# Norms of layer 3's expert rows computed beside layer 0's scatters instead of inside layer 3's attention loop

## The reference, cut to what matters

```python
x = x + L0_xattn(layernorm(x), ctx, mask)        # 16 heads of 8
x = x + L0_ffn(layernorm(x))   # self-attention, then 16 experts, top 2, with a capacity of 128 tokens each
x = x + L1_xattn(layernorm(x), ctx)              # 8 heads of 64
x = x + L1_ffn(layernorm(x))                     # two-token attention, 8 experts, top 1
x = x + L2_xattn(layernorm(x), ctx)              # 16 heads of 64, normed queries and keys
x = x + L2_ffn(layernorm(x))                     # self-attention, 8 experts and a shared one
x = x + L3_xattn(layernorm(x), ctx)              # 16 heads of 64
x = x + L3_ffn(layernorm(x))                     # 8 experts with weight norm, top 2
```

```python
def _wn(v, g):
    n = sqrt(sum(v * v, axis=-1)); return v / maximum(n, 1e-12) * g[:, None]
for i in range(8):
    W1, W2 = _wn(w1_v[i], w1_g[i]), _wn(w2_v[i], w2_g[i])   # (512, 128), (128, 512)
    h = (x * mask_i) @ W1.T + b1[i]; h = h * sigmoid(h)
    out += mask_i * (h @ W2.T + b2[i])
```

## Time and profile before

| | us |
|---|---|
| median of 3 runs | 1207.38 (1205.71 to 1211.97) |
| profiled execution | 1199.52 |
| its span | 1197.6 |
| PE busy | 948.9 |
| VectorE (DVE) busy | 559.4 |
| ScalarE (ACT) busy | 440.2 |
| GpSimd (POOL) busy | 241.8 |

### The profile page before, as it was taken

One profiled execution on the slowest core, in us unless ns is written; L12 is line 12 of the kernel. 1 busy time (PEld: TensorE's weight loads), 2 busy tenths in 40 slices (PEclk: granted clock), 3 DMA queues, 4 the chain that ended last, 5 costly groups with the idle time before them and its releaser, 6 DMA issues. The chain is left out here.

```text
span 1197.6 us, 15552 instructions
## 1 busy us (share of the span) xinstructions
PE 948.9 (79%) x5561; PEld 645.1 (54%) x5561; DVE 559.4 (47%) x1292; ACT 440.2 (37%) x769; POOL 241.8 (20%) x283
## 2 busy tenths in 40 slices
PE   6976899525728549999768768998699978869998
PEld 4653445324625336777548733232366677747776
DVE  5865446241236452111766747773354537531111
ACT  2431555302313114343443325766222334323443
POOL 0542301041053000000374334100000013430110
PEclk9986879957968858999998877999899989978999
DMA  8005310104520000110000051300011102100111
GB/s 326 1 14 119 116 46 10 37 26 125 164 70 1 1 0 18 36 35 18 1 1 1 1 132 49 93 21 2 1 40 39 49 18 64 61 1 18 36 35 36
DMA packets 33263, 55.71 MB, mean 47 GB/s; under 512 B 3696, under 2 KB 25397, under 8 KB 32816
## 3 DMA queue, kind: packets, MB, share of 16 engines
q1 hardware_dynamic: 32176, 52.88, 14.5%
q0 software_dynamic: 1024, 1.98, 0.6%
HBM read 44.81 MB, written 9.96 MB: 46 GB/s over the span
## 5 line engine op out<-in xcount | busy, mean ns | idle before, releaser
L2312 PE MATMUL psum<-xT_all,wexp 128*128 128x512 f32 x400 | 184.7, 607 | 1.3 <-issue 0.7
L1511 DVE TENSOR_REDUCE arena<-psum 128x2 f32<-128x1024 f32 (+3 forms) x128 | 127.2, 1021 | 73.5 <-PE psum L2098 46.0
L1058 ACT ACTIVATE arena<-psum 128x512 f32<-128x512 f32 (+3 forms) x256 | 116.1, 516 | 83.8 <-PE psum L2111 45.3
L743 POOL TENSOR_TENSOR rstd<-var,held 128x4 f32<-128x4 f32 (+3 forms) x30 | 54.2, 1820 | 392.7 <-DVE var L1267 372.0
L2312 PEld LDWEIGHTS psum<-xT_all,wexp 128*128 128x128 f32 x400 | 74.6, 196 | 78.8 <-issue 73.8
L2012 PE MATMUL psum<-values_out_all,arena 128*128 128x128 f32 x560 | 80.1, 293 | 36.8 <-ACT arena L1022 27.6
L2327 PEld LDWEIGHTS psum<-wexp,arena 128*128 128x128 f32 x800 | 95.9, 195 | 15.0 <-issue 14.8
L2095 PE MATMUL psum<-arena 72*128 72x512 bf16 (+3 forms) x256 | 83.0, 396 | 24.4 <-DVE arena L1511 11.8
L814 POOL TENSOR_TENSOR arena<-arena,small 128x616 f32<-128x616 f32 x56 | 67.9, 1216 | 147.8 <-DVE small L1451 147.4
L2327 PE MATMUL psum<-wexp,arena 128*128 128x128 f32 x800 | 96.2, 278 | 0.0
L2012 PEld LDWEIGHTS psum<-values_out_all,arena 128*128 128x128 f32 x560 | 70.7, 201 | 45.2 <-ACT arena L1022 35.0
(11 more groups left out here) (288 smaller groups left out, 1426.3 us busy)
## 6 DMA issues: line engine op xcount, KB each, us to landing
wexp<-experts SPq DMA_DIRECT2D x32, 514.0 KB, 3.5
parts_k<-wexp SPq DMA_DIRECT2D x12, 384.0 KB, 2.9
arena<-parts_k SPq DMA_DIRECT2D x48, 96.0 KB
arena<-parts_q SPq DMA_DIRECT2D x48, 96.0 KB
arena<-experts SPq DMA_DIRECT2D x8, 514.0 KB, 3.8
wexp<-experts SPq DMA_DIRECT2D x9, 384.0 KB, 3.1
held<-packed SPq DMA_DIRECT2D x1, 2375.0 KB, 15.4
held<-packed SPq DMA_DIRECT2D x1, 2264.5 KB, 20.3
```

The lines of the kernel that those rows point to most:

```text
L743: pool.tensor_tensor(dst, src, half[0:src.shape[0], 0:n], ALU.pow).then_inc(done, 1)
L1058: act.activation(p_self[:, n % 2, kt % 2, j, lo:S], bank(t_bank("keys", c, k), lo, S), ACT.Exp, scale=DS ** -0.5).then_inc(ut_ok, 1)
L1511: dve.tensor_reduce(top[:, x % 2, qt, j:j + 2], src, AX_X, ALU.max, negate=True).then_inc(us_ok, 1)
L2312: mm(bank(c, 0, BANK), wexp[:, side, c * P:(c + 1) * P], xT_all[:, b * S:(b + 1) * S], start=True, stop=True).then_inc(h_ps, 1)
```

## The change

The eight experts' rows go into layer 0. After the last value matmul of layer 0's self-attention and after the loads of experts 2 and 3, SyncE loads 1024 columns of each of layer 3's eight experts into `rows3`, the first 8192 columns of the arena, by eight DMAs of 512 KB. ScalarE, behind layer 0's gating, waits for all eight (`n_in`), squares them in place and then loads the Gelu table. PE, behind the bias matmuls and the wait for `b2_ok`, sums the squares by the same 64 matmuls, all into bank 7, expert after expert, before it starts on the queues. VectorE takes the two maxima for all experts at once before its first queue; POOL takes three powers behind its 16 scatters. In layer 3's loop squares, sums, maxima and powers are gone, and so are the eight loads before it; experts 0 and 1 are loaded once, at the end of layer 2. The semaphore counts are adapted.

```diff
 # SyncE, layer 0
             for side in range(2, 4):
                 load0(side, side)
+            for e in range(8):
+                sp.dma_start(rows3[:, e, :], experts[3][e][:, 0:1024]).then_inc(n_in, 16)
             sp.wait_ge(scattered, 16 * 16)
...
-                if l == 3:
-
-                    for side in range(2):
-                        sp.wait_ge(ye_ps, 2 + KB[l])
-                        load(l, side, side)
-                    with sp.Fori(0, 3) as i:
-                        for side in range(2):
-                            sp.wait_ge(n_sq, i * 2 + (side + 1))
-                            load(l, i * 2 + (side + 2), side)
-                    sp.wait_ge(n_sq, 8)
-                else:
-                    sp.wait_ge(ye_ps, 2 + KB[l])
+                sp.wait_ge(ye_ps, 2 + KB[l])
...
 # POOL
-            def inverse_norms(n):
-
-                pool.wait_ge(n_max, 2 + 2 * (n + 1))
-                for v in (s1_all[:, 8 * n:8 * n + 8], s2_col[:, 2 * n:2 * n + 2]):
+            def inverse_norms():
+
+                pool.wait_ge(n_max, 1)
+                for v in (s1_all[:, 0:16], s1_all[:, 16:32], s2_col):
                     pool.tensor_tensor(v, v, half[:, 0:v.shape[-1]], ALU.pow).then_inc(n_inv, 1)
...
-                    if l == 3 and n % 4 == 3 and n > 4:
-                        inverse_norms(n // 4 - 1)
-                if l == 3:
-                    inverse_norms(3)
...
                             .then_inc(scattered, 16)
+                inverse_norms()
                 for side in range(4):
...
 # ScalarE
-                def squares(e):
-                    side = e % 2
-                    act.wait_ge(w_in[side], 16 * (e // 2) + 16 * (WB[3][side] + 1))
-                    act.wait_ge(n_ps, e + 1)
-                    act.activation(sq[:, side, :], wexp[:, side, 0:1024], ACT.Square).then_inc(n_sq, 1)
...
-                        if l == 3 and n % 2 == 0:
-                            squares(n // 2)
...
+                for e in range(8):
+                    act.wait_ge(n_in, 16 * 8)
+                    act.activation(rows3[:, e, :], rows3[:, e, :], ACT.Square).then_inc(n_sq, 1)
                 act.preload_act_table(ACT.Gelu)
...
 # VectorE
-                def norms(e):
-                    side = e % 2
-                    dve.wait_ge(n_ps, e + 3)
-                    raw = bank(7, 8 * side, 8 * side + 5)
-                    dve.tensor_scalar(s1_all[:, 4 * e:4 * e + 4], raw[:, 0:4], 1e-24, None, ALU.max)
-                    dve.tensor_scalar(s2_col[:, e:e + 1], raw[:, 4:5], 1e-24, None, ALU.max).then_inc(n_max, 1)
...
+                raw = bank(7, 0, 64).rearrange("p (e c) -> p e c", c=8)
+                dve.wait_ge(n_ps, 8)
+                dve.tensor_scalar(s1_all.rearrange("p (e c) -> p e c", c=4), raw[:, :, 0:4], 1e-24, None, ALU.max)
+                dve.tensor_scalar(s2_col.unsqueeze(2), raw[:, :, 4:5], 1e-24, None, ALU.max).then_inc(n_max, 1)
                 run_queues(dve, (features, 2), (answer, 0))
...
 # PE
-                def norms(e):
-                    side = e % 2
-                    pe.wait_ge(n_sq, e + 1)
-                    pe.wait_ge(n_max, e + 2)
-                    for c in range(8):
-                        at_ = 8 * side + min(c, 4)
-                        last = mm(bank(7, at_, at_ + 1), sq[:, side, c * P:(c + 1) * P],
-                                  w("ones", 0, 1), start=(c <= 4), stop=(c < 4 or c == 7), skip_group_check=True)
-                    last.then_inc(n_ps, 1)
...
-                    if l == 3 and n % 2 and n < 2 * NT:
-                        norms(n // 2)
...
+                pe.wait_ge(ov_ok, GROUPS)
+                for e in range(8):
+                    pe.wait_ge(n_sq, e + 1)
+                    for c in range(8):
+                        at_ = 8 * e + min(c, 4)
+                        last = mm(bank(7, at_, at_ + 1), rows3[:, e, c * P:(c + 1) * P],
+                                  w("ones", 0, 1), start=(c <= 4), stop=(c < 4 or c == 7), skip_group_check=True)
+                    last.then_inc(n_ps, 1)
                 run_queues(pe, (turned, 2), (hidden, 1), (output, 0))
```

More of the change, by code:

```diff
@@ L259, in program @@
         gatesT = M["gT"][0:16, :]
-        sq = two(X["sq"])
+        rows3 = arena[:, 0:8192].rearrange("p (e n) -> p e n", e=8)
         s1_all, s2_col = n_sum[:, 0:32], n_sum[:, 32:40]
@@ L284, in program @@
         ones_set, wide_set, pj_ps, hi_ok, v_in_ok = sems("ones_set wide_set pj_ps hi_ok v_in_ok")
-        k_split, q_split = sems("k_split q_split")
+        k_split, q_split, n_in = sems("k_split q_split n_in")
         part_out = [sem(f"part_out{n}") for n in range(B)]
@@ L528, in load_count @@
         def load_count(l, e, side):
-            before = 16 * (WB[l][side] + (4 if l == 3 else 0) + 1) - 8 * side
+            before = 16 * (WB[l][side] + 1) - 8 * side
             return e * 8 + before
@@ L867, in router_norm3 @@
                 held_in(pool, 4)
-                pool.wait_ge(n_max, 2 + 8 + 1)
+                pool.wait_ge(n_max, 2)
                 gv = small[0:8, 0, 33:34]
@@ L873, in row_norms3 @@
             def row_norms3():
-                pool.wait_ge(n_inv, 2 * TB)
+                pool.wait_ge(n_inv, 3)
                 pool.tensor_tensor(s1_all, s1_all, w("m3_g1"), ALU.mult)
@@ L884, in experts3 @@
                     for side in range(2):
-                        pool.wait_ge(w_in[side], i * 16 + 16 * (WB[3][side] + 4 + 1))
+                        pool.wait_ge(w_in[side], i * 16 + 16 * (WB[3][side] + 1))
                         carry(5 + side)
@@ L1235, in _ @@
             dve.sem_inc(x_done, 2)
-            dve.sem_inc(n_max, 2)
             dve.sem_inc(d_y, 2)
@@ L1451, in xattn @@
                         dve.reciprocal(part(n - 1, 2), part(n - 1, 1)).then_inc(e_inv, 1)
-                    if l == 3 and n % 2 == 0 and 2 <= n < 2 + 2 * NT:
-                        norms(n // 2 - 1)
                     if u is not None:
@@ L1849, in _ @@
             pe.sem_inc(ye_ps, 2)
-            pe.sem_inc(n_ps, 2)
             ident = w("ident")
```

## The result

The changed kernel takes 1197.26 us (median of 7 runs, 1192.61 to 1201.55) against 1205.71 us for the kernel before (7 runs, 1201.61 to 1211.97): a ratio of 0.9932, 95% interval 0.991 to 0.9954. It is faster by 0.7%, 8.4 us between the medians. The forecast was 1202.7 us, 4.7 us less than before; the likeliest case's own range, 1200.4 to 1206.5, ends above the result. The profiled execution of after was the highest of its runs (1201.55 us, span 1199.8), that of before the lowest (1199.52), so the two spans must not be subtracted; the comparison goes stage by stage, each against its own start.

A forecast was written before the change was run, and what follows sets the result against it. TensorE was busy 79% of the span; layer 3's sums and squares stood in its chain of waits. Removing them gains 17.7 us, layer 0 pays 13.0, net -4.7 from 1207.4: 1202.7 us, range 1188 to 1209.

The forecast's parts named there:

- the likeliest case: Whole kernel: 17.7 us gained in layer 3, 13.0 us paid in layer 0, net -4.7 us; chance 0.58.
- The middle and the tail: Layer 3's cross-attention loop: ten middle halves fall from 43.94 to 30.6 us, gain 13.3; tail gains 1.6 us.
- The start: Layer 3's loop, first reduction to sixth half's: 17.40 us falls to 14.6, a gain of 2.8 (2.4 to 4.7).
- The block in layer 0: PE before layer 0's queues: 128 one-column passes at 1.2 GHz take 27.0 us, delaying the queue loop by 13.0 us.
- The 0.2 for the last pass's drain: Layer 0, end of PE's sums: 0.2 us added to the delay for draining the last pass.
- Rival (a): Layer 0: the clock rises some 5 us into PE's norm passes; cost 0.7, net -17.0 us, 1190.4 us; chance 0.27.
- Loads, squares, powers, maxima at 0: Layer 0: eight new loads cost 0 (bound 3 us), squares and powers are hidden; VectorE's maxima were counted at 0.3 us.
- Rival (c): Layer 0: the eight loads delay routing or scatters beyond 3 us; at 6 us the kernel takes 1208.7; chance 0.07.
- Both norms' parts add up in the halves: Layer 3's middle pair: 6.05 + 1.68 + 1.04 = 8.77 us against 8.79 now, so the norms were paid in full.
- rival (d): Layer 3: the halves don't shorten because something else is as late; 13.0 us stand alone, 1220 us; chance 0.02.
- Rival (b): Layer 3's ten middle halves: PE's clock falls, 5.4 us more a pair; two pairs give 1213.6 us; chance 0.06.
- The base: Whole kernel before: median of the runs shown, 1207.4 us, from which the forecast subtracted 4.7 us.

The follow-up runs named there:

- l3_few: Kernel before, with layer 3's sums of squares cut from eight matmuls per expert to one of five columns, squares kept; 1189.25 us, ratio 0.9873.
- wide_ones: Changed kernel with 128 columns of ones instead of one as moving operand of layer 0's 64 matmuls; 1192.57 us, ratio 0.9899.
- skip_sums: Changed kernel with only one of each expert's eight sum matmuls in layer 0, loads, squares, maxima and powers kept; 1183.45 us, ratio 0.9839.
- fold_wide: Changed kernel with VectorE folding each expert's four W2 chunks of squares into one, leaving 80 passes of 128 columns; 1186.94 us, ratio 0.9858.
- late_plain: Changed kernel with its 128 one-column passes moved behind layer 0's last queue, beside the gathers; 1194.78 us, ratio 0.992.
- late_wide: Changed kernel with the 128 passes moved behind layer 0's last queue and made 128 columns wide; 1195.74 us, ratio 0.9941.
- fold_narrow: Changed kernel with VectorE folding each expert's four W2 chunks of squares into one, leaving 80 one-column passes; 1185.88 us, ratio 0.9855.
- l0_only: Kernel before with layer 0's loads, squares, 128 one-column passes and maxima added, layer 3's norms kept; 1218.6 us, ratio 1.0127.
- late_fold_wide: Changed kernel with W2 squares folded on VectorE and the 80 passes of 128 columns moved behind layer 0's last queue; 1183.99 us, ratio 0.9839.

## Why the prediction was right, and where a size was off

**The direction and the mechanism** held: 1197.26 us lies in the range (1188 to 1209), and layer 3's gain and layer 0's price stand where they were forecast. The difference is -8.4 us where -4.7 was forecast. It lies beyond the likeliest case's own end (-7), and so does the gain in layer 3 (20.2 against at most 20.0): the wide range, drawn to take in the rivals, is what covers it.

**The middle and the tail** of layer 3: 13.3 and 1.6 forecast, 13.67 and 1.64 measured. Layer 1's loop was the right price list: its pair of 6.05 us came out to the hundredth. **The start** is the term that was mis-sized: "I take 14.6, a gain of 2.8 (2.4 to 4.7)"; measured 12.47, a gain of 4.9. The reason given for 14.6 was that layer 3's first halves leave PE idle as layers 1 and 2's did. But in before's trace the clock stood at 0.50 when those two loops began, with a mean of 0.78 and 0.77 over the start; in layer 0 it was 1.00. Layer 3 enters at 1.00, before and after, and without its norms it stays there: in all eleven traces of kernels without them the start took 12.46 or 12.47 us at 1.00. Layer 0's row (12.73) was the near one; with it the net would have been -6.6. That row wasn't safe by itself, though. Layer 0 also enters at 1.00 in after, and there the clock fell on the way:

```profile
27.60:42.00 14.40, 11.45 (x52) 7.16 (x51) 11.11 (x18) 4.88 (x7) 6.57 (x5) 0.88 0.00 1
```

So the same start took 12.7 or 14.4 us in layer 0, in parts of the kernel that the change doesn't touch. The clock at entry doesn't decide by itself, and what else does isn't shown. The prediction also read the fall in before's start as the work of the 16 one-column passes; l3_few shows a fall at the same place with two.

**The block in layer 0**: 27.0 us and a cost of 13.0 forecast, 27.46 and 12.8 measured. The 0.2 for the last pass's drain stands in no row, and neither it nor VectorE's 0.3 shows: the first transpose starts 0.1 us before the block's last pass ends, and VectorE's maxima lie beside that transpose. A pass at 0.213 us in place of 0.211 adds 0.3; that the cost came out to 0.2 us is partly luck. Rival (a), that the clock rises under the norms, is wrong for one-column passes and right for 128-column ones (wide_ones). "Activity releases the throttle" (the Trainium skill, TensorE: Matmul & The Clock Gate, "What's actually happening") doesn't hold for this block as it stands: 27 us of PE busy without a gap, at a granted clock of 0.50 throughout.

**Loads, squares, powers, maxima at 0**: skip_sums puts the first queue 14.4 us after the addition. Rival (c) is out. **Both norms' parts add up in the halves** (8.77 against 8.79): a pair takes 6.05 without them, and l3_few gives 1.74 and 1.00 us for the parts; rival (d) is out. **Rival (b)**, the thinned halves let the clock fall: the clock is 1.00 in all three windows.

**The base.** The forecast subtracted 4.7 from 1207.4. Seven runs put before at 1205.71, so 1.7 of the 5.4 us between forecast and result are the base. Of the rest, 2.7 lie in the two stages (-7.4 for -4.7), and about 1.0 isn't assigned.

## What to carry to other kernels

Before moving PE work into a gap, ask at which clock it will run there and whether it will lift that clock itself: here the 128 passes went from 15.4 us in all to 27.5, and 12.8 of 20.2 us gained were given back. Fold on an idle engine first, and look for cover whose end is set by something long: 80 passes cost 3.4 us beside the scatters and nothing that stands out from the variation beside the gathers, against 12.8 for all 128 beside the scatters. When a rule about the clock is read from a row for one stage, run it over every other stage that the change touches, and look at a second trace before taking the row for a price: the same start of a loop took 12.7 or 14.4 us.

## What was not expected of the hardware

**One-column passes and the clock.** A pass of fp32 costs the same with 1 and with 128 columns (11 in 2 us at 1.2 GHz and 20 in 2 us at 2.4 GHz for both), so wider passes are free here; but only the wide ones were followed by a rise of the clock (6 us in), and under narrow ones a clock of 1.00 fell 2 us in (late_plain), where under wide ones at the same place it stayed up for all 108 passes (late_wide).

**PE's instructions can come slowly beside GpSimd's indirect transfers.** With passes at 0.11 us, PE ran short of instructions from 272.3 to 277.2 us (wide_ones), 272.9 to 277.4 (fold_wide) and for the last 20 passes of late_wide, 14.2 us or 0.7 us each; each time it ended 3 to 5 us after the last scatter or gather was issued. With the gathers held back it was gone (14.46 us for 128 passes). It doesn't always come: at 0.213 us a pass, PE ran on beside the same gathers (late_plain) and beside the scatters (after, fold_narrow), but not quite in l0_only (1.2 us), and 80 fast passes that began 3.6 us ahead of them were done at 336.7 without a pause (late_fold_wide). By what path the transfers slow the instructions isn't shown.
